# Attention of the first layer in a two-layer tower: positions and type in one table, other PSUM banks, another order on each engine, another order of the loads

## The reference, cut to what matters

```python
emb = tok_w[input_ids] + pos_w[jnp.arange(S)] + type_w[token_type_ids]
h   = (emb - mean) * gamma * rsqrt(var + EPS) + beta
h   = h + attn0(layernorm(h))      # softmax over the 64 rows of axis 0, 12 heads
h   = h + moe(layernorm(h))        # router, top 2 of 8, 192 -> 768 -> 192
h   = h + attn1(layernorm(h))      # softmax over 128, relative positions
h   = h + tree(layernorm(h))
```

## Time and profile before

| | us |
|---|---|
| median of three runs (1717.68 to 1722.53) | 1720.91 |
| the profiled execution | 1716.83 |
| its span, first to last instruction | 1715.1 |
| attention of layer 0, start to last DVE write | 0 to 434 |
| experts, about | 500 to 1150 |
| attention of layer 1 and tree, about | 1150 to 1715 |

### The profile page before, as it was taken

The page is one execution under the profiler, slowest core; times in us unless marked ns, Lnnn a source line. Parts: engine busy times, 40 slices in busy tenths (PEclk is TensorE's granted clock), DMA queues, the critical chain, the costliest instruction groups (busy, mean ns, idle before and its releaser), DMA issues. The chain is left out here.

```text
span 1715.1 us, 58930 instructions
## 1 busy us (share of the span) xinstructions
PE 1576.5 (92%) x18950; PEld 1439.4 (84%) x18950; DVE 1268.9 (74%) x2908; ACT 1124.7 (66%) x3086; POOL 806.8 (47%) x1457
## 2 busy tenths in 40 slices
PE   3999999999288999999999999679999999999987
PEld 2888888887278999999999999568888888888873
DVE  5899999997784555555555555378899889989876
ACT  2899999998193333433334333288899999999961
POOL 4576667663003222232322322356677776777620
PEclk9999999999598999999999999788999999999987
DMA  4122222222117988888889899286788888888844
GB/s 127 46 73 72 70 70 70 71 72 51 35 37 203 262 252 261 256 256 257 253 258 247 266 257 248 77 220 183 213 227 230 228 223 219 223 222 227 220 117 148
DMA packets 350388, 302.17 MB, mean 176 GB/s; under 512 B 44637, under 2 KB 315442, under 8 KB 350322
## 3 DMA queue, kind: packets, MB, share of 16 engines
q1 hardware_dynamic: 329984, 261.37, 54.5%
q0 software_dynamic: 16032, 37.51, 8.7%
q10 hardware_dynamic: 4306, 2.44, 0.6%
HBM read 208.17 MB, written 93.05 MB: 176 GB/s over the span
## 5 line engine op out<-in xcount | busy, mean ns | idle before, releaser
L1077 ACT ACTIVATE prob<-ps_s,b1s 128x256 f32<-128x256 f32 x426 | 178.8, 471 | 345.3 <-PE ps_s L1044 307.0
L972 POOL DMA_INDIRECT xs<-zn_d,idx x71 | 68.7, 968 | 366.5 <-PE ps_t L1008 364.9
L1044 PE MATMUL ps_s<-xhi,w1hi_c 128*128 128x256 f32 x852 | 236.2, 295 | 1.6 <-ACT xhi L1070 1.6
L1044 PE MATMUL ps_s<-xhi,w1lo_c 128*128 128x256 f32 x852 | 227.1, 284 | 0.0
L1019 PE MATMUL ps_v<-probT,prob 128*128 128x192 f32 x852 | 208.4, 326 | 0.0
L1019 PE MATMUL ps_k<-probT,prob 128*128 128x192 f32 x852 | 208.2, 326 | 0.0
L408 PE MATMUL ps_q<-xT,wqk_c 128*128 128x128 f32 x1536 | 202.8, 284 | 2.2 <-ACT xT L640 2.2
L408 PEld LDWEIGHTS ps_q<-xT,wqk_c 128*128 128x128 f32 x1536 | 194.4, 200 | 5.3 <-ACT xT L640 3.1
L619 ACT ACTIVATE kT<-ps_q,halves 128x128 f32<-128x128 f32 (+1 forms) x512 | 173.0, 366 | 4.9
L1044 PEld LDWEIGHTS ps_s<-xhi,w1hi_c 128*128 128x128 f32 x852 | 164.5, 193 | 2.0 <-ACT xhi L1070 2.0
L1044 PEld LDWEIGHTS ps_s<-xhi,w1lo_c 128*128 128x128 f32 x852 | 164.4, 193 | 0.0
(11 more groups left out here) (225 smaller groups left out, 4180.1 us busy)
## 6 DMA issues: line engine op xcount, KB each, us to landing
rel_d<-rpad SPq DMA_DIRECT2D x64, 864.0 KB
relb<-rel_d SPq DMA_DIRECT2D x64, 768.0 KB, 5.1
probT<-w2h SPq DMA_DIRECT2D x71, 576.0 KB
score<-w1h SPq DMA_DIRECT2D x71, 384.0 KB, 3.4
score<-w1h SPq DMA_DIRECT2D x142, 192.0 KB, 4.5
ys_d<-ys SPq DMA_DIRECT2D x71, 192.0 KB
tok<-b2h SPq DMA_DIRECT2D x71, 96.0 KB
posb<-pos_w SPq DMA_DIRECT2D x128, 48.0 KB, 2.6
```

The source lines that it names most:

```text
L972: pool.indirect_dma_start(xs[b][:, s, :], None, zn_d, bass.IndirectOffsetOnAxis(ap=ix[b][:], axis=0)).then_inc(x_ld[b], 16)
L1044: last = pe.matmul(dst, w, x, start=(k == 0), stop=(k == len(terms) - 1))
L1077: last = act.activation(hT[b][:, c, :], ps_s[:, j, (c % 2) * BLK:(c % 2) * BLK + BLK], ACT.Gelu, bias=b1s[b][:, c:c + 1])
```

## The change

1. **Embedding.** At the start SP loads the 128 position rows and type row 0, DVE adds them once (`base`, in the buffer of `zn[0]`), SP writes the sum to a new tensor `base_d` in DRAM, waits for that, and then fetches each tile's position rows from `base_d`. `typ1` becomes type row 1 minus type row 0. So `embedding` has four parts in place of five: one operation `(typ1 x typf) + e` instead of two.
2. **Banks (layer 0).** Output projection moves from `ps_t` to `ps_k`, `xn` from `ps_s` to `ps_t`, `ts` from `ps_t` to `ps_s`, the second half of the transposed probabilities from `ps_q` to `ps_t`. The waits that guard the banks move with them.
3. **Orders (layer 0).** `sc` has age 5 (was 4), `s` age 6 (was 5). PE, ACT and DVE call their parts in another order.
4. **Loads.** ACT issues the nine loads of layer 0 at once at the start, SP the seven small ones. The 13 loads of layer 1, and `relw` and `rel32s`, go to SP, three behind each of steps 5 to 9, the zeros of `rel_d` behind steps 10 and 11. POOL clears `wout4` and `zrow` behind step 1. DVE's 12 operations on `relw` go into the expert stretch, at its step 5.

```diff
-AGES = [dict(gather=0, emb=1, ln=2, xn=3, qk=4, v=4, sc=4, s=5, pt=6, o=7, on=8, ts=8, y=9, z=10),
+AGES = [dict(gather=0, emb=1, ln=2, xn=3, qk=4, v=4, sc=5, s=6, pt=6, o=7, on=8, ts=8, y=9, z=10),
...
+        ps_pt = [[ps_k, ps_t], [ps_k, ps_q]]
+        ps_y_in = [ps_k[:, 0:D + LOGITS[0]], ps_t[:, 256:256 + D + LOGITS[1]]]
+        ps_x_in = ps_t[:, 0:256]
+        ps_ts_in = [ps_s[:, 1, 0:256], ps_t[:, 0:256]]
...
-                bank_s = lambda: after(pe, S["s_rd" if l == 1 else "s_sub"], done("s"))
+                bank_s = lambda: after(pe, S["s_rd" if l == 1 else "s_sub"], before("sc"))
...
-                    after(pe, S["xT_sb" if l == 0 else "r_sb"], done("xn" if l == 0 else "r"))
+                    after(pe, S["oT_sb" if l == 0 else "r_sb"], done("ts" if l == 0 else "r"))
...
@@ out_project
+                    if l == 0:
+                        after(pe, S["pt_sb"], npt * before("pt"))
...
@@ turn_sums
-                    after(pe, S["y_ok"], done("y") if l == 0 else before("y"))
+                    if l == 0:
+                        bank_s()
...
@@ act_steps, l == 0
-                exponentials()
                     values()
+                    exponentials()
+                    turned_sums()
                     queries()
+                    turned_inputs()
                     keys_out()
-                    turned_inputs()
                     if st.has("pt"):
+                        turned_probs(1)
                         turned_probs(0)
-                        turned_probs(1)
-                    turned_sums()
...
@@ embedding
-                        marks["e"] = ch.step(dve.scalar_tensor_tensor(e, typ0[:], typn[:, bass.ds(te, 1)], e,
+                        marks["e"] = ch.step(dve.scalar_tensor_tensor(e, typ1[:], typf[:, bass.ds(te, 1)], e,
                                                                       ALU.mult, ALU.add))
-                        marks["e"] = ch.step(dve.scalar_tensor_tensor(e, typ1[:], typf[:, bass.ds(te, 1)], e,
-                                                                      ALU.mult, ALU.add))
...
@@ block_a.sync
-            for dst, src in [(ids, ids_h), (typi, typ_h)]:
-                sp.dma_start(dst[:], src).then_inc(ids_ld, 16)
...
+            sp.dma_start(ids[:], ids_h).then_inc(ids_ld, 16)
+            sp.dma_start(base[:], pos_w[0:B, :]).then_inc(table_ld, 16)
+            sp.dma_start(typ0[:], type_w[0:1, :].to_broadcast([128, D])).then_inc(table_ld, 16)
+            sp.dma_start(typi[:], typ_h).then_inc(row_ld, 16)
+            for dst, src in [(typ1, type_w[1:2, :]), (gam, gamma), (bet, beta)]:
+                sp.dma_start(dst[:], src.to_broadcast([128, D])).then_inc(row_ld, 16)
+            sp.wait_ge(base_ok, 1)
+            sp.dma_start(base_d, base[:]).then_inc(base_st, 16)
+            sp.wait_ge(base_st, 16)
...
+            def behind(n):
+                if 5 <= n <= 9:
...
+                    for dst, src in late[3 * (n - 5):3 * (n - 4)]:
+                        sp.dma_start(dst, src).then_inc(late_ld, 16)
+                if 10 <= n <= 11:
...
+                    sp.dma_start(heads[:, :, LPAD + REL:2 * B - 1], zrow[:].rearrange("p (h c) -> p h c", h=H))\
+                        .then_inc(rel_zero, 16)
```

More of the change, by code:

```diff
@@ L113, in pipeline @@
         body(Step(ages, n, n // 2, n % UNROLL, tiles))
+        if behind:
+            behind(n)
     at0 = links.at if links else 0
@@ L291, in tower @@
         const_ld = dsem("const")
-        N_CONST = 15
+        N_CONST = 9
         ids_ld = dsem("ids")
+        table_ld = dsem("table")
+        row_ld = dsem("row")
+        base_st = dsem("base")
+        base_ok = sem("base_ok")
+        base = zn[0]
         late_ld = dsem("late")
-        N_LATE = 13
+        N_LATE = 15
         pool_c = sem("pool_c")
@@ L403, in queries_keys @@
                     after(pe, S["k_sb"], before("qk"))
-                    after(pe, S["pt_sb"], npt * before("pt") - (1 if npt == 3 else 0))
+                    if l == 1:
+                        after(pe, S["pt_sb"], npt * before("pt") - 1)
                     for j in range(2 * SLOTS):
@@ L473, in turn_sums @@
                     after(pe, S["oT_sb"], before("ts"))
-                    after(pe, S["y_ok"], done("y") if l == 0 else before("y"))
-                    if l == 1:
+                    if l == 0:
+                        bank_s()
+                    else:
+                        after(pe, S["y_ok"], before("y"))
                         after(pe, S["xT_sb"], before("xn"))
-                    pe_transpose(pe, ps_t, on[st.two("ts")][:]).then_inc(S["oT_ps"], 1)
+                    pe_transpose(pe, ps_ts_in[l], on[st.two("ts")][:]).then_inc(S["oT_ps"], 1)
                 def relative():
@@ L497, in turn_inputs @@
                     if l == 0:
-                        bank_s()
+                        after(pe, S["pt_sb"], npt * before("pt") - 1)
                     else:
@@ L518, in body @@
                         sums(1)
-                    if st.has("ts"):
-                        turn_sums()
+                    if st.has("pt"):
+                        turn_probs(0)
+                    if st.has("sc"):
+                        scores()
                     if st.has("pt"):
@@ L545, in body @@
                         sums(1)
-                if st.has("sc"):
-                    scores()
+                    if st.has("sc"):
+                        scores()
             pipeline(pe, ages, body, behind=behind)
@@ L1186, in body @@
                         .then_inc(D_["xlo_sb"], 1)
+                if isinstance(st.n, int) and st.n == 5:
+                    rw = relw[:].rearrange("p (a g j) -> p a g j", a=A, g=G)
+                    dve.wait_ge(late_ld, 16 * N_LATE)
+                    for g in range(G):
+                        q = slice(32 * g, 32 * g + 32)
+                        for a in range(A):
+                            half = odd_half(g, a)
+                            ins = dve.tensor_scalar(rw[q, a, g], rw[q, a, g], rel32s[q, half:half + 1], None,
+                                                    ALU.subtract)
+                    ins.then_inc(dve_c, 1)
                 if st.has("y"):
```

123 lines of the change are left out of this document (59 added, 64 removed).

## The result

| | us |
|---|---|
| changed kernel, median of 4 runs (1699.74 to 1706.39) | 1704.37 |
| kernel before beside it, median of 4 runs (1717.68 to 1724.69) | 1721.72 |
| ratio, with its 95% interval | 0.9901 (0.9882 to 0.992) |
| the profiled execution of the changed kernel, its span | 1706.06, 1704.2 |

The change gains 1%, some 17 us. 1708 was forecast: right in size. To see where the time comes from, I take the same events out of both traces (starts on PE and DVE, us from the start of the span; "v" is the product for the values, one per tile). "Changed, again" is a second profiled execution of the same changed kernel, which ran beside the last experiments.

The account below looks back on a forecast made before the run. PE alone was taken as the bound, at 5.94 us a tile. Terms -2.5 + 0.5 - 6.8 - 4.5 + 0.5 = -12.8 us took 1720.9 to 1708.1 us; range 1696 to 1717, the forecast case's own 1701 to 1714.

Parts of the forecast that it names:

- The forecast case: Whole kernel: -12.8 us to 1708.1 us, own range 1701 to 1714, chance 0.68.
- PE alone needs 5.94 us and DVE as much: Layer 0 steady steps: PE's own work takes 5.94 us a tile, DVE happens to need as much; relieving DVE alone frees nothing.
- I cost it at 0: Layer 0 embedding: the removed DVE operation, 0.33 to 0.41 us a tile on DVE, gains 0 because PE covers it.
- Rival A: Layer 0 steady steps: DVE was the bound after all, another 0.2 us a tile, -12 us, 1696; chance 0.09.
- The order of PE: Layer 0 steady steps: cheaper passages between full array and small tiles, step of 5.90 us, -2.5 us, bounds -5 to +3.
- The term "+0.5" for the turn: Loop turn on PE: branch behind transposes instead of scores, up to 0.04 us more for each of 13 turns, +0.5 us.
- New waits of PE: Layer 0 steady steps: PE's new waits for DVE and ACT are all hidden with 0.7 us or more, cost 0.
- rival C: Layer 0 steps: ACT becomes the bound, meeting PE twice a step; at 0.5 us +5, 1726; chance 0.06.
- The start: Start of layer 0: with the moved loads gone, first v at 21.9 instead of 28.73, -6.8 us, bounds -3 to -9.
- the trip of `base_d`: Start: SP's write of `base_d` takes 2.8 us or more to land, fetching rows 2.8 more; first embedding at about 12.
- The ramp: Four early steps: scores no longer wait for ACT's copy of xn, 22.9 us instead of 27.85, -4.5 us, bounds 0 to -7.
- What was moved: Late loads and zeros behind steps 5 to 11: +0.5 us, bounds 0 to +4; `relw` operations in the expert stretch: 0.

Follow-up runs that it names:

- the orders alone: The kernel before with only the new banks, ages and orders, keeping its loads and three-operation embedding: ratio 1.0047 (1.0033 to 1.0062).
- the loads alone: The kernel before, its banks, ages and orders kept, with the changed kernel's loads and two-operation embedding: ratio 0.9988 (0.997 to 1.0005).
- norm ahead: The kernel before with two DVE calls exchanged, `normalised_rows()` ahead of `embedding(0)`: ratio 0.9986 (0.997 to 1.0002).
- shorter start: The changed kernel with position rows of tiles 0 to 3 straight from `pos_w`, `base_d` stored behind step 2, POOL's clears behind step 0: 1700.03 us, 0.9888.

## Why the prediction was right, and which of its steps were not

The forecast case came out: 1704.4 where 1708 was the likeliest, in its own range. That the sum came so near is in part luck: the largest term, the start, rests on moved loads that turned out not to be needed, the turn has the wrong sign, and the parts do not add up one by one as the sum has them. Against the changed kernel's first execution, step by step:

| step | forecast | measured | from |
|---|---|---|---|
| first v | -6.8 | -5.1 (again: -6.3) | 28.73 to 23.60 |
| ramp of four steps | -4.5 | -5.5 | 27.85 to 22.35 |
| order of PE, turn, moved loads | -1.5 | -4.5 | fifth to last v, 355.34 to 350.81 |
| drain | 0 | +0.3 | last v to routing, 22.50 to 22.76 |
| `relw` in the experts | 0 | +0.2 | first to last product, 560.88 to 561.09 |

**PE alone needs 5.94 us and DVE as much: right.** The kernels with work out of one engine gain 0.01 and 0.17 us a round, the one with work out of both 0.85. The reading of rows 2, that PE's wait at the turn is a wait for DVE, does not hold: it stays with DVE relieved (waits above).

**"I cost it at 0" (the removed operation): right against the kernel before, and wrong as a reading of the change.** The sum came out because the text laid PE's 5.90 us against a DVE of 5.61, which holds only with the operation gone. Put back behind the new orders, and right behind its producer, it costs 16 us and turns the change into none. The step that failed is the one that priced the parts one by one and added them: the orders alone are slower (1.0047), the loads with the shorter embedding nothing (0.9988). The prediction asked of each cost what covers it, and did not ask what covers it after the rest of the change. Rival A ("DVE was the bound after all") falls: with the DVE operation out alone the ratio is 0.9998. The rule beside it (the Trainium skill, Perfetto Trace Analysis, Identifying the Most-Contended Engine) pointed at DVE, 97.7% against the weight loads' 86%; here DVE was one of two full engines.

**The order of PE: the step right, the turn mis-sized.** 5.90 was forecast for a step, 5.89 to 5.90 measured. The term "+0.5" for the turn had the wrong sign. A turn cost 24.17 - 4 x 5.94 = 0.41 us before and 23.81 - 4 x 5.89 = 0.25 after: -0.16 a turn, -2.1 over 13. With scores moved back to the end of the step it is 0.44 again. In every kernel whose steps PE holds, the turn is 0.40 to 0.44 us with scores ahead of it and 0.25 with transposes.

**New waits of PE: "all are hidden with 0.7 us or more": right for this order, and the margin real.** The wait of the second half of pt for ACT's copy of xn is not in my list at all. Its margin is 0.85 us; ACT's old order breaks it and costs 0.63 us a tile. That is the mechanism of rival C with its meeting point, and it did not decide only because ACT's order was changed with the banks.

**The start: size near, mechanism half wrong.** "All that leaves the start" took the moved loads for the cause. With them back at the start the first v is at 22.29, no later. The order on DVE, `xn` ahead of the next embedding, is enough by itself; it stood in the diff, and I read past it. (The chain in the prediction also adds up to 20.0 and not 20.3 for the norm: 12.0 + 6.3 + 2.0 - 0.3.) The first embedding "at about 12" was wrong: 14.54, and 13.27 to 13.73 in the six other kernels and executions with this start. The step that failed is the trip of `base_d`, costed at 2.8 us:

```profile
base_d<-zn SPq DMA_DIRECT2D x1, 96.0 KB, 4.8
```

It landed 4.8 us after its issue (3.7 to 4.2 us in six other executions with this start), while ACT's nine loads were moving. The bounds held 4 us more for this and the clears, and the sum took none of it. The fixed part of about 2.0 us for a transfer (the Trainium skill, DMA: Bandwidth & Descriptors, Anatomy of one DMA, where it is a fit to transfers that GpSimd issues) would have made the trip shorter; it is further off here than the 2.8 us of the row.

**The ramp: right in size and sign.** It needs both halves: 30.2 us with the loads alone, 28.4 with the orders alone, 22.3 with both. Of the loads half it needs neither the 15 late loads moved (22.9 with them back at the start) nor the operation gone (23.9 with it back); which of the rest it needs, the early weights, the position table or the moved `relw` operations, no run tells.

**What was moved: right, +0.5 or less,** but one reason given was wrong: a position row is not issued "two steps (12 us) ahead of use" but one (73.64 and 79.79 above; 70.94 and 77.63 in the changed kernel). With the old orders that is too little behind a write of zeros and DVE stands for 2.90 us; in the changed kernel for 0.6 us. And with all of it at the start again the last v comes at 395.64, no later than in the changed kernel: moving them gained nothing that these runs show.

## What to carry to other kernels

When two engines are equally full, price a change as a whole: what one part costs depends on the others, and here the halves gave -2 (not to be told from 0) and +8 us while the whole gave -17. For each wait that a new bank or order creates, write down the margin in us (here 0.85 us of ACT's copy, 0.28 us of DVE a tile) and ask which old part of the change would eat it. And when an engine stands in a long wait, look first at what is queued behind the waiting instruction on the same engine: exchanging two calls brought the first product forward by 6.4 us with the late transfer as late as ever (2.9 us of it reached the end of the layer).

## What the runs showed of the hardware that I had not expected

- The turn of a loop on PE costs by what stands ahead of it: 0.40 to 0.44 us behind the scores (six kernels), 0.25 us behind three transposes (the changed kernel and two made from it).
- A DVE operation that needs the result of the one right ahead starts 0.45 us after it (0.54 in the kernel with the orders alone), an independent one 0.33 us after.
- A 96 KB store landed 3.7 to 4.8 us after its issue beside nine weight loads, a 48 KB broadcast row in a quieter stretch 2.8 us after the earlier trace rows.
- Time won at the first v is not time won at the last: of 6.4 us 2.9 were left (norm ahead), of 1.3 us 0.3 (shorter start), of 5.1 us nothing (loads alone, 2.4 of them lost in the ramp and the rest at a late position row).
